# Cross attention: VectorE divides one unit's values ahead of an older batch's slot numbers

## The chip, the cores and the metric

One core of a Trainium2 chip runs the whole program. The metric is the device time in microseconds (us), as the median of three runs.

## The reference

Two decoder layers work on x of 8 batches x 256 tokens x 256 features, and on a context of 8 x 77 x 256. Each layer is: layer norm and self attention, layer norm and cross attention against the context, then a mixture of 8 experts. Cut to the cross attention of layer 0 and to the choice of experts that follows it:

```python
q, k, v = (query @ wq.T + bq), (key @ wk.T + bk), (value @ wv.T + bv)   # 16 heads of 16
attn = softmax(q @ k.T / sqrt(16)); ctx = attn @ v
x = x + ctx @ wo.T + bo
gate_logits = layernorm(x) @ Wg.T            # 8 experts
top_v, top_i = top_k(gate_logits, 2)         # two experts a token, gated by a softmax over the two
```

Layer 1 has the same cross attention with other weights, and its own top-2 experts.

## The kernel before, in words

The program is a row of stages: attention of layer 0 (L0a), cross attention (L0x), experts (L0f), and the same for layer 1 (L1a, L1x, L1f). The change is in `attention_crossed`, which writes both L0x and L1x. Each engine has a queue of instructions in an order written out by hand, and the engines meet only at semaphores.

**Units.** A batch b has two units, u = 2b (its *first* unit, c = 0) and u = 2b + 1 (its *second*, c = 1), each with 8 of the 16 heads; units run from 0 to 15. A unit goes through these steps, and all engines work on neighbouring units at once:

- TensorE makes scores (line 827). VectorE takes maxima (`maximum`, 468). TensorE turns them (837), and VectorE subtracts them from the queries (`shift`, 475).
- TensorE makes the scores again with keys as rows (`turned_scores`, 850). ScalarE takes exponentials (667). TensorE makes values and sums of the weights (`values`, 865) in the one bank `ps_o`.
- VectorE divides: `sums(u)` is a reciprocal (480) and a product (483), and frees `ps_o`.

TensorE's order in a first unit u is: scores(u+1), turning of u's maxima, the query product of b+1 (300), `r0` of b-2 (804), `values(u-1)`, `turned_scores(u)`. In a second unit it is: `r1` of b-2 (809), scores(u+1), turning, the value product of b+1 (288), the projection `o` of b-1 (797), transposes of b+2 (293), `turned_scores(u)`, `values(u-1)`, `r2` of b-2 (815). `o(b-1)` waits for `sums(2b-1)`, and `values(u)` for `sums(u-1)`.

**Routing.** Batches that are done are routed in the same queues, a part in each unit. VectorE's `choose` finds the two experts of a batch (514 to 529), `add` adds the projection to X and takes statistics (498 to 506), and `slots` counts tokens of each expert and makes the rows' slot numbers (536 to 546). GpSimd turns statistics into factors (255 to 258). ScalarE normalises the rows (`route_norm`, 627), and TensorE's `r0`, `r1` and `r2` make the logits and the counts. GpSimd's `send` (744) scatters a batch's rows into a table in device memory, in four indirect DMAs that wait for `slots`. Behind them in its queue is `bias` (725), one 128x512 addition in SBUF. `route_norm(b)` writes into the buffer that `send(b-2)` read, and waits until that scatter has landed.

**VectorE's order** is that of the function below. In a first unit of b >= 3 it is: `maximum(u+1)`, `shift(u)`, keys in u = 7 and 8 (192), statistics of b+2 (178 to 183, until b = 5), `slots(b-3)`, a piece of the experts' list, and `sums(u-1)`. The piece is at b = 3 a first count (L0x alone), at b = 5 the `order` of the experts (and in L0x `last_at_least`), at b = 6 and 7 a `snapshot`. When `order` is done, SyncE loads the first experts' weights.

Of the kernel before, what the change touches and what calls it, by code (L numbers as in the profile page):

```python
# [309 lines left out]
def attention_crossed(nc, name, env, wo, bo, first, route, experts, final):  # L310
# [10 lines left out]
    BANKS, PITCH, units, K_GROUPS, REST, TAIL, turns, at, events, by_scalar, keys_made, part, of, mid, START, END = first["order"]  # L321
# [22 lines left out]
    with ExitStack() as stack:  # L344
# [51 lines left out]
        def bank(*turn):  # L396
            if turn in TAIL:
                return ps_o if turn in (("r1", B - 2), ("r2", B - 2), ("r1", B - 1)) else ring[:, spare, :]
            return ring[:, at[turn] % BANKS, :]
# [40 lines left out]
        with nc.Block(no_gpsimd_drain=True) as block:  # L440
# [18 lines left out]
            def _(eng):  # L459
                def linked(ins):  # L460
                    first["linked_v"](eng, ins)

                def maximum(u):
                    eng.wait_ge(scores_done, u + 1)
                    for r0, i, n in runs(u):
                        src = ring[:, i:i + n, 0:4 * SC].rearrange("p n (g k) -> p n g k", k=SC)
                        dst = tops[u % 2][:, :, 2 * DH * r0:2 * DH * (r0 + n):2 * DH].rearrange("p g n -> p n g")
                        eng.tensor_reduce(dst, src, AX.X, ALU.max, negate=True).then_inc(max_done, 1)  # L468

                def shift(u):  # L470
                    b, c = part(u)
                    eng.wait_ge(tops_turned, u + 1)
                    eng.wait_ge(q_out, 3 * (b + 1))
                    q = q_m[b % 2][:, c, :, :]
                    eng.tensor_tensor(q, q, bank("m", u)[:, :].rearrange("p (w s) -> p w s", w=HALVES), ALU.add).then_inc(shifted, 1)

                def sums(u):
                    b, c = part(u)
                    eng.wait_ge(values_done, u + 1)
                    linked(eng.reciprocal(rsum[:, :], ps_o[:, S:2 * S]))  # L480
                    if c == 0 and b:
                        eng.wait_ge(projected, b)
                    eng.tensor_tensor(o_t[:, c, :], ps_o[:, 0:S], rsum[:, :], ALU.mult).then_inc(o_out, 1)
# [9 lines left out]
                def add(b):  # L493

                    eng.wait_ge(projected, b + 1)
                    eng.wait_ge(biased, b + 1)
                    xb = X[:, b * QT_N:(b + 1) * QT_N, :]
                    eng.tensor_tensor(xb, xb, bank("o", b)[:, :].rearrange("p (q d) -> p q d", q=QT_N), ALU.add).then_inc(added, 1)
                    eng.wait_ge(added, b + 1)
                    for q in range(QT_N):  # L500
                        ins = eng.bn_stats(r_stats[:, q, :], X[:, b * QT_N + q, :])
                    linked(ins)
                    if b:
                        eng.wait_ge(r_rstd_done, b)
                    for q in range(QT_N):
                        ins = eng.bn_aggr(r_mv[:, q, :], r_stats[:, q, :])
                    ins.then_inc(r_var_done, 1)

                def choose(b):

                    par = b % 2
                    wait_out(eng, "r1", b)
                    for q in range(QT_N):
                        ins = eng.max(top[:, q, :], logits[:, q, :])
                    linked(ins)
                    if b:
                        eng.wait_ge(odds_done, b)
                    eng.tensor_tensor(apart[:, :], top[:, :, 1], top[:, :, 0], ALU.subtract).then_inc(apart_done, 1)
                    for q in range(QT_N):
                        ins = eng.max_index(index[:, q, :], top[:, q, :], logits[:, q, :])  # L520
                    linked(ins)
                    linked(eng.tensor_copy(index_f[:, :, :], index[:, :, 0:TOP]))
                    for k in range(TOP):
                        ins = eng.tensor_tensor(chosen[:, k, :, :], route["experts"][:, :].unsqueeze(1).to_broadcast([P, QT_N, EXPERTS]),
                                                index_f[:, :, k].unsqueeze(2).to_broadcast([P, QT_N, EXPERTS]), ALU.is_equal)
                    linked(ins)
                    eng.tensor_tensor(both[:, :, :], chosen[:, 0, :, :], chosen[:, 1, :, :], ALU.add).then_inc(both_done, 1)
                    eng.tensor_copy(xr[:, par, :, FIRST_EXPERT], index_f[:, :, 0])
                    eng.tensor_copy(xr[:, par, :, TOKEN], route["from_end"][:, b * QT_N:(b + 1) * QT_N])

                def slots(b):

                    par, taken = b % 2, route["taken"]
                    eng.wait_ge(odds_done, b + 1)
                    gate = xr[:, par, :, GATE:GATE + TOP]
                    linked(eng.tensor_scalar(first_gate[:, :], odds[:, :], 1.0, None, ALU.add))
                    linked(eng.reciprocal(gate[:, :, 0], first_gate[:, :]))
                    eng.tensor_tensor(gate[:, :, 1], gate[:, :, 0], odds[:, :], ALU.mult)
                    wait_out(eng, "r2", b)
                    for q in range(QT_N):  # L540
                        eng.tensor_tensor(place[:, q, :], counts[:, 0, q, :], taken[:, :], ALU.add)
                        linked(eng.tensor_tensor(taken[:, :], counts[:, 1, q, :], taken[:, :], ALU.add))
                    linked(eng.tensor_tensor(picked[:, :, :, :], chosen[:, :, :, :],
                                             place[:, :, :].unsqueeze(1).to_broadcast([P, TOP, QT_N, EXPERTS]), ALU.mult))
                    linked(eng.tensor_reduce(slot_f[:, :, :], picked[:, :, :, :], AX.X, ALU.add))
                    eng.tensor_copy(slot_i[:, par, :, :], slot_f[:, :, :].rearrange("p k t -> p t k")).then_inc(slot_done, 1)
# [5 lines left out]
                for u in range(units):  # L552
                    b, c = part(u)
                    if u == 0:
                        shift(0)
                    if u + 1 < units:
                        maximum(u + 1)
                    if u:
                        shift(u)
                    for t in mid(u):  # L560
                        if t[0] == "k":
                            first["take_keys"](eng, t, bank(*t))
                    if c == 0:
                        if b + 2 < B:
                            first["statistics"](eng, b + 2)
                        if b >= 3:
                            slots(b - 3)
                            if b == 3 and not final:
                                experts["count_first"](eng)
                            if b - 3 == ORDER_BY:  # L570
                                experts["order"](eng)
                                if not final:
                                    experts["last_at_least"](eng)
                            for i, last in enumerate(FULL_BY):
                                if b - 3 == last:
                                    experts["snapshot"](eng, last)
                    else:
                        if b >= 2:
                            choose(b - 2)
                        if u == units - 1:  # L580
                            sums(u - 1)
                        if b >= 1:
                            add(b - 1)
                    if u and u < units - 1:
                        sums(u - 1)
                slots(B - 3)
                x["take_early"](0)
# [2204 lines left out]
```

## Time and profile before

| | |
|---|---|
| median of 3 runs | 1499.4 us (1499.39 to 1502.16) |
| the profiled execution's own time | 1493.69 us |
| its span, first to last instruction | 1492.0 us |
| mean granted TensorE clock | 0.991 |
| busy in the span: TensorE | 1419.1 us (95%) |
| busy in the span: VectorE | 754.9 us (51%) |
| busy in the span: ScalarE | 625.6 us (42%) |
| busy in the span: GpSimd | 493.2 us (33%) |

Shares are means over stages with different limits, so the two stages that the change touches have to be read for themselves. Batches 3 to 7 lie at about 261 to 343 us in L0x and at 1116 to 1198 us in L1x. A start in the rows is us from the span's start.

### The profile page before, as it was taken

The page shows a single profiled execution, that of the slowest core. Times are in us where ns is not written, and L with a number is a line of the kernel's source. Part 1 is how long each engine was busy: PE and PEld are TensorE (multiplying, and loading weights), DVE is VectorE, ACT ScalarE, POOL GpSimd, SP SyncE. Part 2 cuts the span into 40 slices and gives each one's busy share as a digit, 9 for nine tenths or more (in the row PEclk, how much of TensorE's full clock was granted, in tenths as well). Part 3 has the DMA queues.
Part 4 walks back from the last instruction along what each step waited for, and adds up shares of the span by engine and source line. Part 5 has one row for each costly group of instructions (what it writes and reads, how often), then busy time and mean ns, then how long its engine had stood idle before and what let it go on. Part 6 is the DMA issues. An engine that isn't in the chain of part 4 may idle for free. (4 is left out here: it accounts for less than half of the span.)

```text
span 1492.0 us, 33834 instructions
## 1 busy us (share of the span) xinstructions
PE 1419.1 (95%) x11400; PEld 1146.9 (77%) x11401; DVE 754.9 (51%) x2161; ACT 625.6 (42%) x1726; POOL 493.2 (33%) x758
## 2 busy tenths in 40 slices
PE   7999989989999999999999999999899999999998
PEld 5666666667999999967777777777666679999997
DVE  6777757997333333344444444444378962222222
ACT  3444446653122222245454554554366543333332
POOL 3555532445212212223323322333124452222222
PEclk9999999999999999999999999999899989999999
DMA  9930000152243333210000000000001522534332
GB/s 319 343 107 25 23 16 16 44 178 80 37 147 93 91 88 95 37 53 1 1 1 1 1 1 1 0 1 1 1 16 45 186 76 36 148 93 96 94 90 34
DMA packets 84464, 101.35 MB, mean 68 GB/s; under 512 B 11483, under 2 KB 77379, under 8 KB 84355
## 3 DMA queue, kind: packets, MB, share of 16 engines
q1 hardware_dynamic: 64643, 77.58, 16.3%
q0 software_dynamic: 13680, 17.19, 6.7%
q10 hardware_dynamic: 6032, 5.12, 1.0%
q8 instruction: 69, 1.13, 0.3%
q14 instruction: 40, 0.33, 0.1%
HBM read 57.51 MB, written 39.59 MB: 65 GB/s over the span
## 5 line engine op out<-in xcount | busy, mean ns | idle before, releaser
L1784 POOL TENSOR_TENSOR L1a_prob<-L1a_prob,L1a_rtot 128x1024 f32<-128x1024 f32 x64 | 121.1, 1892 | 277.4 <-DVE L1a_rtot L1657 277.4
L2313 PEld LDWEIGHTS L0x_ps<-L0f_rows_t,L0f_w_up 128*128 128x128 f32 x1584 | 182.0, 192 | 10.4 <-issue 9.0
L2313 PE MATMUL L0x_ps<-L0f_rows_t,L0f_w_up 128*128 128x128 f32 x1584 | 184.2, 276 | 5.6 <-issue 4.8
L2389 ACT ACTIVATE L1f_hid<-L1x_ps,L1f_b_up 128x128 f32<-128x128 f32 x296 | 92.8, 364 | 164.2 <-PE L1x_ps L2313 163.8
L2313 PEld LDWEIGHTS L1x_ps<-L1f_rows_t,L1f_w_up 128*128 128x128 f32 x1184 | 140.2, 194 | 3.4 <-issue 1.6
L2313 PE MATMUL L1x_ps<-L1f_rows_t,L1f_w_up 128*128 128x128 f32 x1184 | 141.1, 278 | 0.6 <-ACT L1f_rows_t L2373 0.6
L2322 PE MATMUL L1x_ps<-L1f_w_down,L1f_hid 128*128 128x256 f32 x592 | 135.8, 383 | 1.9 <-DVE wv L2491 1.9
L2257 POOL TENSOR_TENSOR turn<-eps 128x1 f32<-128x1 f32 x74 | 13.6, 184 | 374.3 <-DVE wv L2491 370.7
L1726 ACT ACTIVATE L1a_prob<-L1a_ps_s,L1a_nmax 128x256 f32<-128x256 f32 x256 | 118.4, 474 | 38.5 <-DVE L1a_nmax L1652 38.5
L2322 PEld LDWEIGHTS L1x_ps<-L1f_w_down,L1f_hid 128*128 128x128 f32 x592 | 110.7, 192 | 16.0 <-issue 2.1
L1287 POOL TENSOR_SCALAR_AFFINE_SELECT L0a_prob<-L0a_prob 128x128 f32<-128x128 f32 (+1 forms) x256 | 82.4, 362 | 90.7 <-ACT L0a_prob L1219 90.7
L2381 ACT ACTIVATE ctx_in<-L0x_ps 128x256 f32<-128x256 f32 x72 | 27.6, 384 | 181.5 <-PE L0x_ps L2313 181.4
L2322 PE MATMUL L0x_ps<-L0f_w_down,L0f_hid 128*128 128x256 f32 x432 | 99.4, 380 | 1.5 <-DVE L0f_hid L2478 1.5
L1652 DVE TENSOR_REDUCE L1a_nmax<-L1a_ps_s 128x2 f32<-128x512 f32 x128 | 79.4, 682 | 32.2 <-PE L1a_ps_s L1848 32.2
L1219 ACT ACTIVATE L0a_prob<-L0a_ps 128x384 f32<-128x384 f32 x128 | 52.4, 496 | 98.9 <-PE L0a_ps L1373 98.9
L2322 PEld LDWEIGHTS L0x_ps<-L0f_w_down,L0f_hid 128*128 128x128 f32 x432 | 79.3, 190 | 11.0 <-DVE L0f_hid L2478 1.7
L1862 PEld LDWEIGHTS L1a_ps_t<-ident,L1a_prob 128*128 128x128 f32 x500 | 59.6, 141 | 34.6 <-issue 26.3
L2478 DVE TENSOR_TENSOR L0f_hid<-ctx_in,L0x_ps 128x256 f32<-128x256 f32 x72 | 30.2, 421 | 104.6 <-ACT ctx_in L2381 104.6
L1862 PE MATMUL L1a_ps_t<-ident,L1a_prob 128*128 128x128 f32 x500 | 76.9, 276 | 3.3 <-DVE L1a_prob_t L1661 2.4
L1661 DVE COPY L1a_prob_t<-L1a_ps_t 128x512 f32<-128x512 f32 x63 | 42.9, 681 | 58.9 <-PE L1a_ps_t L1862 58.9
L1736 ACT ACTIVATE L1a_prob_t<-L1a_ps_t 128x512 f32<-128x512 f32 x62 | 37.1, 598 | 81.4 <-PE L1a_ps_t L1862 81.4
L2468 DVE TENSOR_SCALAR token<-L1f_from_end 128x1 int32<-128x1 f32 x37 | 5.7, 154 | 128.7 <-DMA out_dram<-wv,token 128.7
(490 smaller groups left out, 2794.9 us busy)
## 6 DMA issues: line engine op xcount, KB each, us to landing
expert_table<-zero SPq DMA_DIRECT2D x1, 16640.0 KB, 69.7
L0f_w_up<-in_w_dram SPq DMA_DIRECT2D x8, 1408.0 KB, 6.4
L1f_w_up<-in_w_dram SPq DMA_DIRECT2D x8, 1024.0 KB
L1f_w_down<-in_w_dram SPq DMA_DIRECT2D x8, 1024.0 KB
L0f_w_down<-in_w_dram SPq DMA_DIRECT2D x8, 768.0 KB, 8.3
L1f_rows<-expert_table SPq DMA_DIRECT2D x35, 130.0 KB
L0f_rows<-expert_table SPq DMA_DIRECT2D x32, 130.0 KB
sums<-X SPq DMA_DIRECT2D x8, 256.0 KB, 2.5
```

The lines of the kernel that those rows point to most:

```text
L1219: eng.activation(prob[u % 2][:, r, :, :], bank("p", u, r)[:, 0:KT * W].rearrange("p (t w) -> p t w", t=KT), ACT.Exp).then_inc(exp_done, 1)
L1287: ins = eng.affine_select(out=p, in_=p, compare_op=ALU.is_ge, fill=0.0, base=base, pattern=[[0, 2], [sign, n]], channel_multiplier=-sign)
L1652: eng.tensor_reduce(nmax[:, j % RING, :], src, AX.X, ALU.max, negate=True).then_inc(max_done, 1)
L1661: eng.tensor_copy(prob_t[s % 2][:, k, :], turn_bank(b, s, k)).then_inc(even_out, 1)
L1726: ins = eng.activation(prob[:, j % RING, q, :], ps_s[:, k, q * S:(q + 1) * S], ACT.Exp, bias=nmax[:, j % RING, q:q + 1], accum_out=total[: ...
L1736: eng.activation(prob_t[s % 2][:, k, :], turn_bank(b, s, k), ACT.Copy).then_inc(odd_out, 1)
L1784: eng.tensor_tensor(v, v, r.unsqueeze(2).to_broadcast([P, 2 * QT_N, S]), ALU.mult).then_inc(norm_done, 1)
L1862: ins = eng.transpose(out[:, o:o + P], prob[:, j % RING, q, c * P:(c + 1) * P], ident[:, :])
L2313: ins = eng.matmul(ps_h[c][:, o:o + P], w_up[par][:, t, w0:w0 + P], rows_t[:, t, :], start=(t == 0), stop=(t == DT - 1))
L2322: ins = eng.matmul(ps_y[:, 0:D], hid[:, c, k * P:(k + 1) * P], w_down[par][:, 2 * c + k, :], start=(c == 0 and k == 0), stop=(c == CHUNKS ...
L2389: ins = eng.activation(hid[:, c, k * P:(k + 1) * P], ps_h[c][:, k * P:(k + 1) * P], ACT.Gelu, bias=b_up[par][:, 2 * c + k:2 * c + k + 1])
L2478: ins = eng.tensor_tensor(hid[:, c, :], mid[:, c, :], ps_h[c][:, 2 * P:4 * P], ALU.mult)
```

## The change

In a first unit from b = 3 on, `sums(u-1)` comes ahead of `slots(b-3)` and the piece behind it. In batches 1 and 2 and in second units the order stays as it was. No instruction is added or taken away; the order changes in five units of each of the two stages.

```diff
                     if c == 0:
                         if b + 2 < B:
                             first["statistics"](eng, b + 2)
+                        if u:
+                            sums(u - 1)
                         if b >= 3:
                             slots(b - 3)
...
-                    if u and u < units - 1:
+                    if c == 1 and u < units - 1:
                         sums(u - 1)
```

## Rows read from the trace of the kernel before

**Rows 1.** Busy us (instructions) of PE, PEld, DVE, ACT, POOL; clock, DMA; batch 5

```profile
1149.00:1165.00 16.00, 14.89 (x171) 10.41 (x174) 15.17 (x52) 9.31 (x20) 7.92 (x13) 1.00 0.43 125
```

**Rows 2.** Line 483, who waited for it: us in total, times

```profile
  PE L0x_ps L797: 3.0, 2
...
  PE L1x_ps L797: 1.7, 2
```

**Rows 3.** Timeline, VectorE, L1x batch 3: start, us, instruction, idle before

```profile
1121.04 0.14 DVE L536 TENSOR_SCALAR L1x_first_gate<-L1x_odds 128x2 f32<-128x2 f32 x1
...
1122.49 0.17 DVE L546 CAST L1x_slot_i<-L1x_slot_f 128x4 int32<-128x4 f32 x1
...
1129.04 0.78 DVE L192 TENSOR_SCALAR L_shared<-L1x_ps,half_mask,L1x_k_bias 128x154 f32<-128x154 f32 x2 [2.09 <-PE L1x_ps L282]
...
1130.49 0.17 DVE L522 CAST L1x_index_f<-L1x_index 128x4 f32<-128x4 uint32 x1
```

**Rows 4.** Timeline, TensorE, L1x: the values of units 5, 9, 11 and 13

```profile
1120.74 1.05 PE L865 MATMUL L1x_ps_o<-L1x_prob,half_ones 77*32 77x256 f32 x16
...
1153.76 1.05 PE L865 MATMUL L1x_ps_o<-L1x_prob,half_ones 77*32 77x256 f32 x16
...
1170.35 1.05 PE L865 MATMUL L1x_ps_o<-L1x_prob,half_ones 77*32 77x256 f32 x16
...
1185.00 1.05 PE L865 MATMUL L1x_ps_o<-L1x_prob,half_ones 77*32 77x256 f32 x16
```

**Rows 5.** Timeline, VectorE, L1x batch 5: slots, sums, maximum, shift, a cast of choose

```profile
1154.30 0.13 DVE L536 TENSOR_SCALAR L1x_first_gate<-L1x_odds 128x2 f32<-128x2 f32 x1
...
1157.84 1.75 DVE L480 RECIPROCAL L1x_rsum<-L1x_ps_o 128x256 f32<-128x256 f32 x1
...
1159.97 1.50 DVE L468 TENSOR_REDUCE L1x_tops<-L1x_ps 128x4 f32<-128x308 f32 x2
1161.38 0.68 DVE L475 TENSOR_TENSOR L1x_q_m<-L1x_q_m,L1x_ps 128x512 f32<-128x512 f32 x1
...
1162.76 0.17 DVE L522 CAST L1x_index_f<-L1x_index 128x4 f32<-128x4 uint32 x1
```

**Rows 6.** Timeline, GpSimd, L1x: bias of batch 4; first send and bias of batch 6

```profile
1145.76 1.28 POOL L725 TENSOR_TENSOR X<-X,bo 128x512 f32<-128x512 f32 x1
...
1171.64 1.07 POOL L744 DMA_INDIRECT expert_table<-L1x_xr,L1x_slot_i  x1 [4.74 <-DVE L1x_slot_i L546]
...
1176.52 1.28 POOL L725 TENSOR_TENSOR X<-X,bo 128x512 f32<-128x512 f32 x1
```

**Rows 7.** Timeline, VectorE, L1x batch 4: the same cast of choose

```profile
1145.30 1.79 DVE L522 CAST L1x_index_f<-L1x_index 128x4 f32<-128x4 uint32 x1
```

**Rows 8.** Timeline, TensorE, L1x: r0 of batches 2 and 4; turned scores of 11, 13, 15

```profile
1135.89 0.63 PE L804 MATMUL L1x_ps<-ident,L1x_xr 128*128 128x128 f32 x4 [0.27 <-ACT L1x_xr L627]
...
1162.53 1.10 PE L850 MATMUL L1x_ps<-L1x_q_m,L_shared 32*77 32x256 f32 x16
...
1168.94 0.60 PE L804 MATMUL L1x_ps<-ident,L1x_xr 128*128 128x128 f32 x4
...
1177.59 1.10 PE L850 MATMUL L1x_ps<-L_shared 32*77 32x256 f32 x16
...
1191.34 1.10 PE L850 MATMUL L1x_ps<-L1x_q_m,L_shared 32*77 32x256 f32 x16
```

**Rows 9.** Timeline, ScalarE: the rows' normalisation of batch 4, in L1x and in L0x

```profile
1167.17 1.09 ACT L627 ACTIVATE L1x_xr<-X,L1x_r_shift_by,L1x_r_rstd 128x256 f32<-128x256 f32 x2 [0.89 <-DMA expert_table<-L1x_xr,L1x_slot_i]
...
312.13 1.09 ACT L627 ACTIVATE L0x_xr<-X,L0x_r_shift_by,L0x_r_rstd 128x256 f32<-128x256 f32 x2 [0.61 <-POOL L0x_r_shift_by L258]
```

**Rows 10.** Timeline, VectorE, L1x batch 6: slots, sums of unit 11, shift of unit 13

```profile
1169.71 0.16 DVE L536 TENSOR_SCALAR L1x_first_gate<-L1x_odds 128x2 f32<-128x2 f32 x1
...
1172.09 1.75 DVE L480 RECIPROCAL L1x_rsum<-L1x_ps_o 128x256 f32<-128x256 f32 x1
...
1175.89 0.68 DVE L475 TENSOR_TENSOR L_shared<-L_shared,L1x_ps 128x512 f32<-128x512 f32 x1
```

## The prediction, made before the changed kernel ran

> **What bounds the kernel now.** I read the table of busy time by stretch first. In batch 5 of L1x [rows 1] VectorE is busy for 15.17 of 16 us and TensorE for 14.89. Both are nearly full, so neither has room for a delay. VectorE's queue here is slots, order, sums, maximum, shift, with no idle time between them [rows 5]: it sets the pace, and what it delivers late TensorE waits for. Then I read who waited for the product of `sums`: TensorE's projection `o` did, twice in each stage, 3.0 us in L0x and 1.7 us in L1x [rows 2]. These are the waits that the change aims at. Last come the timelines of the four engines, with two questions. Are the values there when VectorE asks for them earlier? And what stands behind the work that is made later?
>
> **What the change moves.** It adds and removes nothing. Its first effect is `sums` ahead of slots. Its second is that slots, and all that hangs on it, come later: the four indirect DMAs on GpSimd's queue, GpSimd's `bias` behind them, `route_norm` on ScalarE (it waits for a scatter of two batches before), and at batch 5 SyncE's loads of weights. `maximum` and `shift` of the next unit stand behind slots and sums in either order, so they gain nothing; they lose whatever VectorE now idles while it waits for values that slots used to cover.
>
> The prices that recur are these. From the start of a sums to the next instruction VectorE takes 2.13 us (1157.84 to 1159.97) [rows 5]. Slots takes 1.62 us until the slot number is written (1121.04 to 1122.66) [rows 3]. Slots and order take 3.54 us (1154.30 to 1157.84) [rows 5], slots and snapshot 2.38 us (1169.71 to 1172.09) [rows 10]. The maximum before a shift is 1.41 us (1159.97 to 1161.38) [rows 5]. A first send starts 0.3 us after the slot number (written 1.64 us after 1169.71), and bias 4.88 us after that (1171.64 to 1176.52) [rows 6, 10]: 5.2 us from slot number to bias. VectorE starts a reciprocal 0.06 us after its values end, which is my estimate from the near coincidence of such pairs.
>
> **Batch 3, L1x.** The values of unit 5 end at 1121.79 [rows 4], VectorE is free at 1121.04 [rows 3]. It idles 0.8 us, and sums starts at 1121.85. Slots starts at 1123.98 and writes at 1125.6, where it was 1122.66: 2.9 us later. The 0.8 us itself costs nothing, since VectorE waited 2.09 us for a key product after this [rows 3]; without that cover it would cost 0.8. But bias moves to 1130.8 to 1132.1. A cast in batch 4 took 1.79 us instead of 0.17 [rows 3, 7]: it began 0.46 us ahead of the record of bias and ended 0.05 us behind its end (1145.76 + 1.28) [rows 6]. So GpSimd's addition holds small SBUF work of VectorE, from about half a microsecond before its record. In batch 3 the same cast stands at 1130.49 [rows 3], now inside such a stretch (1130.2 to 1132.1): 1.43 us lost. It sits ahead of `add`, and `add` leads over GpSimd and ScalarE to TensorE's r0(2), which already waited 0.27 us for it [rows 8]. TensorE enters batch 4 some 1.4 us late.
>
> The Trainium skill, "SBUF — State Buffer", section "Who interferes with whom", says that VectorE and GpSimd share a port pair under an exclusive lock, taken by whichever starts first, and that a cast or an operation with two SBUF inputs contends while one with at most one does not. The long cast agrees with the kinds it names, but by the records it started first and still waited. By the rule with recorded starts, the cast would pass here and the comparison behind it would be held, at nearly the same price.
>
> **Batch 4.** The old stall of 1.62 us (1.79 less 0.17) [rows 3, 7] goes, because bias moves behind `choose`. VectorE catches up, TensorE does not: it is dense here, and VectorE's lead ends in a wait for values. I take 1.45 us late for TensorE on entry to batch 5 (from below 0, if the cast of batch 3 is missed).
>
> **Batch 5, L1x.** The values of unit 9 ended at 1154.81 [rows 4], now at 1156.26. Sums starts at 1156.32, slots at 1158.45; behind slots and order maximum starts at 1162.0 and shift at 1163.4, ending at 1164.1. Turned scores of unit 11 started at 1162.53 [rows 8], now at 1164.15: 1.6 us late. The projection gets its operand early and no longer waits, but shift is the next thing late, and takes the gain. The slot number is written at 1160.07, bias is at 1165.2, and the cast of `choose` moves from 1162.76 [rows 5] to 1164.8, again inside the held stretch, until 1166.6. The scatter and the weight loads both move 4.1 us (the slot number from 1155.92, 1.62 us after 1154.30). ScalarE's normalisation of batch 4 ended a wait for that very scatter at 1167.17 [rows 9]; it moves to 1171.3. TensorE's r0(4) follows at 1172.5 (1.09 us, and 0.14 to start), where it was 1168.94 [rows 8]: 3.5 us late.
>
> **Batches 6 and 7, L1x.** The values of unit 11 ended at 1171.40 [rows 4], now at 1174.95. Sums starts at 1175.0, and behind it and 2.38 us of slots and snapshot come the maximum (1.35 us, one instruction now) and, at 1180.9, shift, where it was 1175.89 [rows 10]. It ends at 1181.5. Turned scores of unit 13 move from 1177.59 [rows 8] to 1181.65: 4.1 us. Up to here a held operation in batch 6 is saved, but TensorE sets the next values. In batch 7 r0(5) is late by 4.55 us, since bias holds GpSimd until then. So the values of unit 13 end at 1190.6 instead of 1186.05 [rows 4], sums starts at 1190.66, shift at 1195.2, and it ends at 1195.9. Turned scores of unit 15 start at 1195.95 instead of 1191.34 [rows 8]: **4.6 us** for L1x.
>
> **L0x.** The same steps give the same 1.45 at the entry and 1.6 at unit 11. In L0x the normalisation of batch 4 was released by GpSimd and not by the scatter [rows 9]. The late `add` (2.0 us of order and shift, 0.9 of a held operation) puts it 2.9 us late, and a shift of the scatter by 4.1 could at most put it 4.1 late. TensorE had about a microsecond of room, which leaves 2.1 to 3.2; I take 2.4, near the lower end, because that row shows no wait for the DMA. Unit 13 adds 0.5 as in L1x, unit 15 another 0.6: **3.5 us**. What follows each stage is dense TensorE work, which gives nothing back. I expect the later scatters before the early experts to be hidden.
>
> **Sum.** 3.5 + 4.6 = 8.1 us. The profiled execution's own time is 1493.69 us (span 1492.0), so it would be 1501.8. The runs' median lies 5.7 us above that execution, so the median becomes 1499.4 + 8.1 = **1507.5 us**, slower by 0.54%.
>
> **Rivals.**
> - *The cast of batch 3 escapes* (its margin to the start of the held stretch is 0.3 us). Then TensorE enters batch 5 on time, and the same steps end about 2.1 us late in L0x and 3.15 in L1x: 5.3 us, 1504.7. Against it: the stretch is 1.9 us long, and the operations behind the cast would fall into it.
> - *Scatter and bias are absorbed*, so only the idle time for values stays: 0.2 us at unit 11 and 0.5 at unit 13 in each stage, 1.5 us, 1500.9. For it: four operations of batch 4 to 7 that were held are freed. Against it: the DMA wait in L1x [rows 9] is already open, and its source moves.
> - *Faster: the projection's wait is last.* If shift were in time, the waits of 3.0 and 1.7 us [rows 2] would go, 4.7 us: 1494.7. It decides if shift(11) ends before the transposes ahead of turned scores do. Before, shift ended at 1162.06 and the product started at 1162.53 [rows 5, 8], a room of 0.47 us; with the wait gone TensorE asks 0.9 us sooner, and VectorE comes at least 0.5 us later, since it idles for values. Only a freed operation of 1.6 us could tip that.
> - *Worse:* further casts are held, or late scatters reach the early experts' rows. Another 3 us: 1510.5.
>
> **Chances.** My forecast with its neighbourhood (6.5 to 9.5) has 0.40, the escape 0.24, absorbed 0.14, faster 0.10, worse 0.12. The range from 1500.5 to 1511 leaves out the faster case and half of the worse one. A measurement here tells 0.2%, 3.0 us, from no change. Slower by more: forecast, escape and worse, less some of the escape, 0.75. Within: 0.15. Faster by more: 0.10.
>
> **What the profile after would show.** In each first unit of batch 3 to 7 VectorE idles for line 865 ahead of line 480, 0.2 to 1.9 us. `o` waits for line 483 no more, and turned scores (850) wait for line 475 in units 11, 13 and 15. The cast at line 522 is long in batches 3 and 5 and short in batch 4. Line 627 of batch 4 in L1x waits for the scatter some 4 us later than before. The prediction is wrong if VectorE is at line 475 of unit 11 no later than before, or if its held operations vanish altogether.

## The result, and the profile after

The changed kernel took 1512.4 us as the median of six runs (1510.43 to 1514.5), the kernel before 1500.78 us beside it. The ratio is 1.0069, with a 95% interval of 1.0046 to 1.0092: slower by 0.7%. The forecast was 1507.5 us with a range to 1511. The sign and the place of the loss are as forecast, the median lies 1.4 us above the range.

The profiled execution took 1512.99 us, span and clock are these (before: 1492.0 us, 0.991):

```profile
core 0: 1511.3 us, clock 0.983
```

**The wait that the change aims at.** The product of `sums` (line 483), who waited for it, in total us and times; it answers to [rows 2]:

```profile
  PE L1x_ps_o L867: 2.3, 1
  PE L0x_ps_o L867: 2.3, 1
```

The projection `o` is gone from the list. The one wait left in each stage is that of `values`, line 867 (865 before; lines behind the change are two further on), at the very end of the stage. The kernel before had that one too, 1.62 us in each stage where it is 2.3 us now.

**VectorE in L1x**, from batch 3 to batch 5 (start, us, instruction, idle time before it):

```profile
1126.09 1.76 DVE L480 RECIPROCAL L1x_rsum<-L1x_ps_o 128x256 f32<-128x256 f32 x1 [1.28 <-PE L1x_ps_o L867]
...
1140.62 1.67 DVE L522 CAST L1x_index_f<-L1x_index 128x4 f32<-128x4 uint32 x1
...
1142.85 0.68 DVE L498 TENSOR_TENSOR X<-X,L1x_ps 128x512 f32<-128x512 f32 x1
```

They answer to [rows 3]. VectorE now idles for the values ahead of a sums, and the cast of batch 3, 0.17 us before, is held to 1.67 us. The GpSimd addition beside it:

```profile
1139.97 0.96 POOL L746 DMA_INDIRECT expert_table<-L1x_xr,L1x_slot_i  x1 [0.30 <-issue]
1140.96 1.29 POOL L727 TENSOR_TENSOR X<-X,bo 128x512 f32<-128x512 f32 x1
```

The cast starts 0.34 us ahead of the addition's record and ends 0.04 us behind its end (1142.25), as in [rows 6, 7].

**TensorE in L1x**, its waits from batch 4 on:

```profile
1143.59 0.61 PE L817 MATMUL L1x_ps<-L1x_both,before 128*128 128x16 f32 x2 [1.18 <-DVE X L498]
...
1177.70 1.10 PE L852 MATMUL L1x_ps<-L1x_q_m,L_shared 32*77 32x256 f32 x16 [1.05 <-DVE L1x_q_m L475]
...
1185.95 0.63 PE L806 MATMUL L1x_ps<-ident,L1x_xr 128*128 128x128 f32 x4 [1.29 <-ACT L1x_xr L629]
...
1211.97 1.10 PE L852 MATMUL L1x_ps<-L1x_q_m,L_shared 32*77 32x256 f32 x16 [0.93 <-DVE L1x_q_m L475]
```

`r2` waits for the add behind the held cast, turned scores wait for shift at units 11 and 15, `r0(4)` waits for the normalised rows. These rows answer to [rows 8]. The normalisation itself, in L0x and in L1x, answers to [rows 9]:

```profile
317.83 1.09 ACT L629 ACTIVATE L0x_xr<-X,L0x_r_shift_by,L0x_r_rstd 128x256 f32<-128x256 f32 x2 [1.27 <-DMA expert_table<-L0x_xr,L0x_slot_i]
...
1184.72 1.09 ACT L629 ACTIVATE L1x_xr<-X,L1x_r_shift_by,L1x_r_rstd 128x256 f32<-128x256 f32 x2 [3.15 <-DMA expert_table<-L1x_xr,L1x_slot_i]
```

In both stages ScalarE's last wait is now the one for the scatter.

**What no step of the forecast has.** The busy times by stretch show the granted clock in the column after POOL (the columns are those of [rows 1]):

```profile
230.00:310.70 80.70, 74.53 (x833) 52.87 (x837) 68.22 (x178) 50.71 (x107) 29.64 (x53) 1.00 0.11 35
310.70:320.90 10.20, 10.20 (x74) 6.49 (x67) 7.53 (x21) 3.43 (x8) 1.93 (x5) 0.50 1.01 383
320.90:344.80 23.90, 21.34 (x239) 14.15 (x238) 18.14 (x61) 11.59 (x25) 7.58 (x10) 1.00 0.24 78
1096.30:1143.60 47.30, 44.87 (x517) 31.67 (x517) 38.81 (x91) 30.76 (x63) 14.32 (x27) 1.00 0.07 24
1143.60:1150.40 6.80, 6.80 (x33) 5.63 (x34) 4.98 (x8) 1.29 (x3) 1.34 (x4) 0.50 0.13 41
1150.40:1188.00 37.60, 34.18 (x389) 23.80 (x391) 31.08 (x93) 23.41 (x48) 15.76 (x26) 1.00 0.38 119
1188.00:1198.20 10.20, 10.20 (x63) 7.12 (x54) 8.11 (x28) 2.82 (x7) 4.35 (x5) 0.50 0.61 205
```

For 10.2 us of L0x and for 6.8 and 10.2 us of L1x TensorE had 1.2 GHz, where it has 2.4 GHz in the rest. In the profiled execution of the kernel before, these two stages, up to the turned scores of unit 15, ran at 1.00 throughout. That is one execution, with a mean clock of 0.991; other runs of that kernel lie between 0.980 and 0.997. The low stretches begin behind waits of TensorE: the one at 1143.6 with the end of r2's wait of 1.18 us, the one at 310.7 after waits of 1.59 and 0.73 us, the one at 1188.0 some 2 us after a wait of 1.29 us. What half the clock means is seen on one group of products, the query product, in the stretch at 1143.6:

```profile
1146.80 3.62 PE L300 MATMUL L1x_ps<-L1x_xt,wq 128*128 128x256 f32 x8
```

Eight products of this shape take 1.89 us at the full clock; the projection's row at 1158.34, in the experiments below, shows it.

**Where the time went.** From the first sums of a stage to the turned scores of unit 15 the kernel before took 106.4 us in L0x and 105.1 in L1x, the changed one 114.9 and 115.6. That is 8.5 and 10.5 of the 19.3 us between the two spans; the rest of the program adds 0.3. Two executions of unlike clock (0.991 and 0.983) can't tell how much of it is the schedule.

### The profile page after: what moved, and what is told of

It is laid out like the page before. It is cut to its first block and busy times, and to the rows that moved or that the text cites. A ratio compares the mean times of both kernels' runs of the same rounds, so it can differ in the third digit from the quotient of the medians.

```text
span 1511.3 us, 33834 instructions
## 1 busy us (share of the span) xinstructions
PE 1433.3 (95%) x11400; PEld 1154.8 (76%) x11401; DVE 753.7 (50%) x2161; ACT 626.1 (41%) x1726; POOL 494.6 (33%) x758
## 3 DMA queue, kind: packets, MB, share of 16 engines
q8 instruction: 69, 1.13, 0.3%
```

## Telling schedule from clock

All runs but the six of the kernel before in the first call list a time and a mean granted clock, 260 runs in all. The runs of the kernel before alone reach from 1485 to 1511 us, and their time follows the clock. A straight line was fitted, with a constant for each kernel in each call (a group of versions measured together on one chip) and one slope for all. By it a run takes 1.14 us more for each 0.001 of clock that it lacks (standard error 0.02), and what is left over scatters by 1.1 us. The differences between those constants are the times at equal clock below. They compare kernels of one call, on one chip: by the fit the kernel before had 1482.2 us at full clock on one chip and 1487.1 to 1487.8 on the three others. The first row of the table is weaker than the rest. The kernel before lists no clock in that call, so the next call's constant of another chip, 1487.5, stands in; with the 1482.2 of the one fast chip the same row would be 12.6. The ± of the other rows is the standard error of the fit.

| kernel | runs | ratio, 95% interval | mean clock, before's | at equal clock, us |
|---|---|---|---|---|
| changed, first | 6 | 1.0069 (1.0046 to 1.0092) | 0.9847, not listed | +7.3, by a stand-in |
| changed, second | 6 | 1.0121 (1.0096 to 1.0147) | 0.9852, 0.9926 | +8.8 ± 0.6 |
| changed, third | 12 | 1.0073 (1.0049 to 1.0096) | 0.9863, 0.9880 | +8.2 ± 0.4 |
| in L0x alone | 12 | 1.0042 (1.002 to 1.0065) | 0.9849, 0.9864 | +4.1 ± 0.4 |
| in L1x alone | 12 | 1.0011 (0.9988 to 1.0034) | 0.9878, 0.9864 | +4.8 ± 0.4 |
| in batch 3 alone | 12 | 1.0022 (0.9996 to 1.0047) | 0.9884, 0.9864 | +4.0 ± 0.4 |
| from batch 4 on | 12 | 1.003 (1.0005 to 1.0054) | 0.9873, 0.9864 | +5.5 ± 0.4 |
| changed, bias first | 12 | 1.0049 (1.0028 to 1.0069) | 0.9851, 0.9883 | +5.4 ± 0.4 |
| before, bias first | 12 | 1.0014 (0.9989 to 1.004) | 0.9891, 0.9883 | +3.4 ± 0.4 |
| changed, idle products | 6 | 1.0092 (1.0064 to 1.0119) | 0.9895, 0.9883 | +16.3 ± 0.5 |
| before, idle products | 6 | 1.013 (1.0101 to 1.0159) | 0.9873, 0.9883 | +20.9 ± 0.5 |
| sums behind slots | 12 | 1.0008 (0.9992 to 1.0024) | 0.9911, 0.9926 | -0.8 ± 0.4 |
| and the piece behind shift | 6 | 1.0061 (1.0038 to 1.0083) | 0.9855, 0.9926 | +0.9 ± 0.6 |
| changed, piece behind shift | 6 | 1.0123 (1.0102 to 1.0144) | 0.9822, 0.9926 | +6.2 ± 0.6 |
| piece behind choose | 12 | 1.0033 (1.0007 to 1.006) | 0.9849, 0.9880 | +2.8 ± 0.4 |
| piece behind add | 12 | 1.0032 (1.0007 to 1.0057) | 0.9847, 0.9880 | -0.4 ± 0.4 |

## The experiments

### One stage at a time

```diff
-                        if u:
+                        if u and b >= 3 and not final:
                             sums(u - 1)
```

(For the other stage it is `and final`. The condition on the later `sums(u - 1)` is changed to match.)

> The change in L0x alone. Two theories stand. Cascade: each stage pays for itself by held casts, idle time of VectorE and late shifts, so L0x alone costs about half of the change's 10 to 12 us, 5 to 6 us, its last sums come 10 us later than before and L1x takes as long as before. Clock: the extra beyond my 8 us is TensorE's clock, which falls to the half inside the stage; then the half-clock stretch near 310 us is here too and none between 1090 and 1190 us. If instead the execution of before that was profiled was only a lucky one for the clock, the ratio is below 1.002.

> The change in L1x alone. Cascade: 5 to 6 us more, none of it in L0x. Half-clock stretches inside L1x (near batches 4 and 6) as in the changed kernel, none inside L0x. L0x alone and L1x alone should add up to the whole change within 2 us.

At equal clock L0x costs 4.1 us where the forecast had 3.5, and L1x 4.8 where it had 4.6. That is a little under the 5 to 6 us which the expectations gave each. The two together make 8.9, the whole change 8.2 and 8.8 in the calls that list both clocks: the stages add up, and both terms of the sum are near their size. The ratio of the L1x version does not show its 4.8 us, since its clock was 0.0014 higher than that of the kernel before, which is worth 1.6 us. The expectations of the clock came out in part. With the change in L0x alone a stretch of 6.8 us at half clock begins at 277.40, with the end of a wait of 1.55 us of `r2` that the kernel before did not have; none lies near 310 us or inside L1x. With the change in L1x alone there is one of 3.4 us in batch 3 of L1x, but also one of 13.65 us in L0x, where nothing was changed.

### Batch 3 against the rest

```diff
-                        if u:
+                        if u and b == 3:
                             sums(u - 1)
```

> Sums ahead of slots in batch 3 alone, in both stages. Held cast: the cast of choose at line 522 in batch 3 takes 1.7 to 1.8 us instead of 0.17, TensorE is 1.4 us late from there and VectorE gives nothing back, so each stage costs 1.4 to 3 us, 3 to 6 in all. Rival, that idle time for values is the cost: it is covered here by the wait for the key product, so no more than 0.5 us in all.

> Sums ahead of slots in batches 4 to 7, not in 3. Cascade: without the held cast of batch 3 TensorE enters batch 5 on time, the steps give 2.1 us in L0x and 3.15 in L1x, 5.3 us, and up to 9 if the clock falls in batches 5 and 6 all the same. If the held cast of batch 3 set off everything, at most 2 us.

From batch 4 on the change costs 5.5 us, close to the 5.3 us of the rival in which the cast of batch 3 escapes. Here it did escape, since batch 3 was left alone. Batch 3 by itself costs 4.0, in the expected range of 3 to 6; the forecast's sum gave it 2.8 (8.1 less 5.3). Its cast is held for 1.66 us in L1x. The cast of batch 4, which the whole change frees, is held here as well (1.78 us at 1150.31, 0.17 in the changed kernel). The two parts make 9.5, more than the whole, and fit that.

### GpSimd's addition out of the way

```diff
+                        if b in (3, 4, 5, 6, 7):
+                            bias(b)
                         if b >= 3:
                             send(b - 3)
                     else:
-                        bias(b)
+                        if b not in (3, 4, 5, 6, 7):
+                            bias(b)
```

(In the kernel before the same is done in batches 4, 6 and 7 alone, where its operations were held.)

> The changed kernel with GpSimd's bias ahead of its send in batches 3 to 7, so that the 128x512 addition runs while VectorE is in a reciprocal from PSUM. Hold theory: the casts of choose are short in every batch, the loss at batch 3 is gone, and of the change's 10 to 12 us only 2 to 4 stay (idle time for values, late shift, late scatter). Rival, that late scatter and shift are the cost: 7 us or more stay.

> The kernel before with bias ahead of send in batches 4, 6 and 7 alone, where its choose was held for 1.6, 0.9 and 1.9 us. If these holds cost it something, 1 to 3 us less than before; by my steps TensorE's own work limits the gain to 0.5 us in batch 4 and nothing later, so 0.5 to 1.5 us less, inside what can be told.

The same casts of choose in L1x, in batches 3 to 6 of the changed kernel with bias first:

```profile
1125.03 0.17 DVE L522 CAST L1x_index_f<-L1x_index 128x4 f32<-128x4 uint32 x1
...
1143.33 0.28 DVE L522 CAST L1x_index_f<-L1x_index 128x4 f32<-128x4 uint32 x1
...
1158.97 0.17 DVE L522 CAST L1x_index_f<-L1x_index 128x4 f32<-128x4 uint32 x1
...
1177.49 0.42 DVE L522 CAST L1x_index_f<-L1x_index 128x4 f32<-128x4 uint32 x1
```

None takes 1.7 us any more, with the same instruction in VectorE's queue and only GpSimd's order changed. So GpSimd's addition is what holds the cast. The change then costs 5.4 us instead of 8.4 (the mean of its second and third measurements, weighted by precision, ± 0.3), so the move gives back 3.0 us, compared across chips. The expectations had 2 to 4 us left if holds were the cost, and 7 or more if late scatter and shift were; 5.4 lies between them, so each has a part. In the kernel before, the same move was expected to gain 0.5 to 1.5 us and costs 3.4. Bias ahead of the scatters has a price of its own then, and the 3.0 us are what is left after it, so they do not measure the holds alone. That the price comes from the indirect DMAs, which stand behind bias in this order, is argued and not shown.

### Idle products where TensorE waits

```diff
+                    if t in (("r0", B - 4), ("r0", B - 3), ("r2", 1)):
+                        idle_products(eng, out, ident, 8)
...
+                        if B - 4 <= t[1] < B - 1:
+                            idle_products(eng, ps_o, ident, 8)
```

Eight products of 128x128 whose results are overwritten, ahead of `r2(1)`, `r0(4)` and `r0(5)` and behind `o` of batches 4 to 6, in both stages.

> The changed kernel with 8 idle products of TensorE at six places where it waits (before r2 of batch 1, before r0 of batches 4 and 5, behind o of batches 4, 5 and 6), some 0.9 us each. Clock theory: inside L0x and L1x the granted clock stays full, the half-clock stretches of 10 us near batch 5 and 6 are gone, and the kernel is 2 to 5 us below the changed one. Rival, that the clock is not what makes it longer: the same as the changed kernel or slower by the products' own time, up to 4 us.

> Control: the same idle products in the kernel before. It had no half clock inside these stages, so it can only lose: 0 to 8 us (12 places of 0.9 us, less the projection's waits of 3.0 and 1.7 us). If it gains, its other runs than the profiled one lost the clock there too.

Busy times by stretch, the changed kernel with idle products, L0x and L1x from the first sums to unit 15:

```profile
230.20:345.20 115.00, 110.71 (x1236) 82.16 (x1236) 94.77 (x265) 65.36 (x141) 39.63 (x68) 1.00 0.22 76
1095.70:1209.80 114.10, 110.73 (x1240) 82.20 (x1240) 93.78 (x259) 63.77 (x135) 39.53 (x68) 1.00 0.24 77
```

The low stretches inside the two stages are gone in this execution, and the mean clock of its runs, 0.9895, is the highest among the versions that contain the whole change (0.9822 to 0.9863 without the products). That fits a low clock that goes with TensorE's idle time there. The control does not fit as well. In the kernel before, the products were expected to cost at most 8 us, and they cost 20.9 at equal clock; its mean clock was 0.9873 against 0.9883. Its profile has 3.4 us at half clock near 310 us and 6.8 us from about 328 us on, in a stage that ran at 1.00 throughout in the profile without them. Nor are the products a remedy: they stand in front of work that is due, and cost the changed kernel 8 us at equal clock, where 2 to 5 us less than the changed kernel were expected.

### Where the projection's wait goes

Five orders of VectorE's queue, each with one more thing out of the way. In the first, slots stay first and sums go ahead of the piece of the experts' list alone:

```diff
                         if b >= 3:
                             slots(b - 3)
+                        if u:
+                            sums(u - 1)
+                        if b >= 3:
                             if b == 3 and not final:
                                 experts["count_first"](eng)
```

> Slots, then sums, then the piece of the experts' list (first count, order, snapshot): the slot number, the scatters and bias keep their old times, and only the piece goes behind sums, in both stages. The product of sums is ready earlier by the piece, 1.9 us at batch 5 and 0.75 at batches 6 and 7. Theory (shift is the next thing late, and it stands behind the same work as before): the projection's waits go, shift(11), shift(13) and shift(15) stay where they were to 0.3 us, and at equal clock the time is that of the kernel before to 1 us. Rival, the projection's wait was the last one: the waits of 3.0 and 1.7 us are gained, -4.7 us. Rival, sums ahead of anything costs: +1 to +3 us.

TensorE in L1x in that version, with VectorE's rows around it:

```profile
1158.34 1.89 PE L800 MATMUL L1x_ps<-wo,L1x_o_t 128*128 128x256 f32 x8
...
1161.55 1.10 PE L853 MATMUL L1x_ps<-L1x_q_m,L_shared 32*77 32x256 f32 x16 [0.88 <-DVE L1x_q_m L475]
```

```profile
1154.91 0.17 DVE L546 CAST L1x_slot_i<-L1x_slot_f 128x4 int32<-128x4 f32 x1
...
1159.31 1.50 DVE L468 TENSOR_REDUCE L1x_tops<-L1x_ps 128x4 f32<-128x308 f32 x2
1160.73 0.68 DVE L475 TENSOR_TENSOR L1x_q_m<-L1x_q_m,L1x_ps 128x512 f32<-128x512 f32 x1
```

In the kernel before, the projection waited 0.86 us here for line 483 (one of the two waits of [rows 2]):

```profile
1160.20 1.97 PE L797 MATMUL L1x_ps<-wo,L1x_o_t 128*128 128x256 f32 x8 [0.86 <-DVE L1x_o_t L483]
```

Now it does not wait, and 1.3 us behind its end the turned scores wait 0.88 us for line 475. The slot number is written at 1154.91, as early in the stage as before, and maximum and shift follow the piece as they did; the wait has moved in full. In L0x the projection's wait of 2.12 us became two, 1.22 for the maximum that frees a bank for the transposes and 0.73 behind them. Only the other wait, 0.89 us in batch 7, found room: there turned scores of unit 15 are 1.0 us earlier in each stage. At equal clock all of it is worth 0.8 ± 0.4 us, and the ratio, 1.0008 (0.9992 to 1.0024), can't tell it from the kernel before.

In the second the piece goes behind maximum and shift too, so that shift gains as well:

```diff
                     else:
+                        if b >= 3:
+                            if b == 3 and not final:
+                                experts["count_first"](eng)
+                            if b - 3 == ORDER_BY:
+                                experts["order"](eng)
...
                         if b >= 2:
                             choose(b - 2)
```

> Slots, then sums, and the piece of the experts' list goes behind maximum and shift of the next unit, ahead of choose. Now shift(11) is earlier by 1.9 us as well as the product of sums, and shift(13), shift(15) by 0.75 us. Theory (projection and shift both set TensorE's pace, one behind the other): now the waits of 3.0 and 1.7 us are gained at least in part, -2 to -4.7 us at equal clock, and less if TensorE's next wait, for scores or the normalised rows, takes its place. Rival, TensorE's own work is the bound here and its waits only move: within 1 us of the kernel before. Choose and what hangs on it come 1.9 us later at batch 5; if that is what counts, slower by 1 to 2 us.

Against the kernel before, each measured from the stage's first sums, the turned scores of unit 11 are 1.1 us early in L1x and 2.2 in L0x. Those of unit 12 are 1.7 us late in both. TensorE between the two, and what VectorE did meanwhile:

```profile
1172.39 0.37 PE L818 MATMUL L1x_ps<-L1x_both,before 128*128 128x16 f32 x2 [0.80 <-DVE L1x_both L527]
```

```profile
1167.77 1.92 DVE L2030 TENSOR_TENSOR wq<-L1r_by_place 128x64 f32<-128x64 f32 x1
...
1172.07 0.17 DVE L527 TENSOR_TENSOR L1x_both<-L1x_chosen 128x16 f32<-128x16 f32 x1
```

`r2` waits 0.80 us for choose, which stands behind the piece (2.07 us in L0x). An instruction of the piece that takes 0.22 us in the changed kernel, at 305.35 us, is held to 1.92. My theory of a gain of 2 to 4.7 us fell; the rival, that the wait only moves, holds with +0.9 ± 0.6.

The third is the change itself with the piece behind shift.

> The change with the piece of the experts' list moved behind maximum and shift of the next unit. The scatters and bias are as late as in the changed kernel (2.1 to 4.1 us), but shift(11) comes 1.9 us sooner than there, shift(13) and shift(15) 0.75 us sooner. If the late slot number and what hangs on it (scatter, normalised rows, held operations) is what costs at batches 6 and 7, and shift only at unit 11, it stays at +4.5 to +6.5 us at equal clock. If the late shift itself were most of it, +1 to +3 us.

It costs 6.2 ± 0.6 us, within the 4.5 to 6.5 of the theory. Taking 1.9 us off the late shift of unit 11 gives back 2.6 of the 8.8 us that the change costs in the same call. The rest stays with the late slot number and what hangs on it (scatter, rows, held casts); this run does not tell these apart.

In the last two the piece goes behind choose, and behind choose and add.

> As the version with the piece of the experts' list behind maximum and shift, but behind choose too, ahead of add. There r2 waited 0.80 us for choose's last product after shift had gained 1.1 to 2.2 us; here choose keeps its old place. Theory (VectorE's queue is full in batch 5, 15.17 of 16 us, and whatever is put off is what TensorE waits for next): add is 1.9 us late, and the next wait is for rows that are normalised from it; within 1 us of the kernel before at equal clock. Rival, choose was the only one that TensorE needed at once: -2 to -3 us.

> The same with the piece behind add too, as the last work of the second unit before its sums. Choose and add keep their old times, and there was 0.32 us of idle time ahead of these sums. Theory: sums(10) is 1.6 us late, and with it maximum(13), so scores or values wait; within 1 us of the kernel before at equal clock. Rival: shift(13) has room, since it is one unit further on, and the gain of the earlier shift(11) stays: -1 to -3 us, and the version beats both kernels.

Behind choose it is +2.8 ± 0.4 us, which neither theory had. Its profile has, in L0x, a wait of `r0` for the normalised rows of 2.01 us at 333.91 (1.12 in the kernel before) and one of turned scores for line 475 of 1.63 at 327.06. At 312.25 TensorE also idles 2.65 us for "issue", which means that the profile shows nothing it waits for. In L1x the same wait of `r0` is as before, 1.15 against 1.13, and TensorE idles 1.40 and 1.04 us for "issue". These idle times stay unexplained. Behind add it is -0.4 ± 0.4, as the theory had it: `values` now wait for line 483 (1.95 us at 315.97, 0.69 at 1174.84). Its ratio, 1.0032, is above 1 all the same, since its mean clock is 0.9847 against 0.9880. No version of the five beats the kernel before by more than 0.2%.

### The changed kernel again

> The changed kernel once more, unchanged. In all runs so far, some 150 of ten kernels, a kernel's time follows its own mean granted TensorE clock by 1.16 us for each 0.001. By that line the change's schedule costs 7.2 us and the rest of its 10 to 11 us is a lower clock (0.9847 against 0.9871). Theory: at equal clock it is again 6.5 to 8 us longer than the kernel before, and its mean clock is again lower by 0.001 to 0.004. Rival, that the lower clock was chance: the same 7 us at equal clock, and a mean clock within 0.001 of the kernel before's, so that the medians differ by 7 to 8 us.

> The changed kernel a third time, for its clock. So far its mean granted clock was 0.9847 and 0.9852 on two chips, and that of the kernel before 0.9864 to 0.9926. If the late units lower the clock, this gives 0.984 to 0.986 again, below the kernel before in the same call by at least 0.001, and +7 to +8.5 us at equal clock. If the clock is the chip's affair, its mean is within 0.001 of the kernel before's.

At equal clock the change costs 8.8 and 8.2 us, and the clock is 0.9852 and 0.9863, below the kernel before's by 0.0074 and 0.0017. The price of the schedule repeats; 8.8 is a little above the expected 6.5 to 8. By the scatter of the runs the first of the two clock differences is clear, and the second is less than twice its standard error. The mean clock of the changed kernel stays within 0.0016 in three calls, while that of the kernel before moves between 0.9864 and 0.9926 over four; so the clock's part of the difference, 2 to 8 us, depends on the chip or the hour.

The third one's L1x ran at 1.00 from the first sums to unit 15, so its profile can be laid on the forecast without the clock. TensorE:

```profile
1150.03 1.10 PE L852 MATMUL L1x_ps<-L_shared 32*77 32x256 f32 x16
...
1174.49 1.10 PE L852 MATMUL L1x_ps<-L1x_q_m,L_shared 32*77 32x256 f32 x16 [1.05 <-DVE L1x_q_m L475]
...
1182.45 0.63 PE L806 MATMUL L1x_ps<-ident,L1x_xr 128*128 128x128 f32 x4 [1.01 <-ACT L1x_xr L629]
...
1191.62 1.10 PE L852 MATMUL L1x_ps<-L_shared 32*77 32x256 f32 x16 [0.42 <-issue]
...
1205.86 0.46 PE L852 MATMUL L1x_ps<-L1x_q_m,L_shared 32*77 32x256 f32 x4 [0.93 <-DVE L1x_q_m L475]
```

The stage began 9.48 us later than in the profile before (first reciprocal at 1095.69 and 1086.21). With that taken off and the starts of [rows 8] subtracted, unit 11 is late by 2.5 us (forecast 1.6), `r0(4)` by 4.0 (3.5), unit 13 by 4.55 (4.1), unit 15 by 5.0 (4.6). Unit 8, whose start before was 1139.06, is late by 1.5 (1.45). Unit 13 has a wait of 0.42 us that the profile puts down to nothing; its shift ends at 1191.57, 0.05 us ahead of it.

L0x can be compared in the same way in the second measurement, which ran at the full clock there until about 335 us. Its start was 0.33 us later. Unit 8 is late by 1.7 us (forecast 1.45), unit 11 by 1.8 (1.6), `r0(4)`, at 317.92, by 3.4 (2.4), and unit 13, at 327.08, by 3.9 (2.9).

## Why the prediction was right, and where it was wrong

- **The projection's wait is not the last one: right.** Line 483 holds up `o` no more, line 475 holds up turned scores by 0.93 to 1.05 us at units 11 and 15 of L1x, and by 0.42 at unit 13, as forecast. The version with sums ahead of the piece alone shows it with everything else in place.
- **The cast of batch 3 is held, that of batch 4 freed, that of batch 5 held again: right in L1x.** 1.67 us in batch 3 here, and 1.66, 0.17 and 1.80 in batches 3 to 5 of the third measurement. In L0x batch 5 holds an operation of the same routine instead, 1.06 us at line 518. With bias first 3.0 us of the price go.
- **TensorE is late by 1.45 behind batch 3: right**, 1.5 at unit 8 in the execution with a full clock.
- **Unit 11 late by 1.6: too little by 0.9 in L1x.** TensorE's lateness did not stay at 1.45. In that execution the values of unit 8 themselves came late: from the turned scores of unit 9 to `r2` behind these values it is 3.84 us, where it was 2.90 in the kernel before. So unit 10 was late by 2.2 already, and sums and shift follow the values (rows below). The 0.28 us in the rows is all that the profile shows as idle, and it names no releaser; what the 0.94 us are stays open. They are there in L1x of five more profiles with sums ahead of slots in batch 4 (3.83 to 4.25 us), and absent in two, the second measurement and the change with the piece behind shift (2.89 and 2.90). In L0x there was one wait more that I had not looked for, the transposes of the batch after next, which need a bank that `maximum(12)` frees: 1.59 us at 308.83.

```profile
1156.72 1.10 PE L852 MATMUL L1x_ps<-L_shared 32*77 32x256 f32 x16
...
1159.95 0.68 PE L867 MATMUL L1x_ps_o<-L1x_prob,half_ones 77*32 77x256 f32 x5 [0.28 <-issue]
1160.56 0.39 PE L817 MATMUL L1x_ps<-L1x_both,before 128*128 128x16 f32 x2
```

- **The scatter leads to `r0(4)`: right in L1x, too small in L0x**, where I had it only as a bound and took 2.4 us. There too ScalarE's idle time ends with the scatter (1.27 us in the first profile), `r0(4)` is 3.4 us late in the second measurement, and L0x costs 4.1 instead of 3.5.
- **The sum, 8.1 us: right at equal clock**, where the two measurements beside a kernel before with a listed clock give 8.8 and 8.2, mean 8.4 ± 0.3. How close it came is in part luck. In L1x the excess of 0.9 us at unit 11 had shrunk to 0.4 at unit 15, and batch 3 alone cost 4.0 where the sum gave it 2.8.
- **"So the median becomes 1499.4 + 8.1": this step failed.** It takes for granted that the clock stays, and so puts the clock's term at nothing without a reason. The runs of the changed kernel had 0.9847, and those of the kernel before in later calls 0.9864 to 0.9926. The median of the kernel before beside it was also 1.4 us above the one I was shown, so the difference in that call is 11.6 us where 8.1 was forecast. With the new median the schedule's 7.3 makes 1508.1, and a clock lower by 0.0017 to 0.0036 (against 0.9864 to 0.9883, the calls with much the same time before) adds 1.9 to 4.1: 1510.0 to 1512.2, where 1512.4 was measured. This reckoning takes the first call's chip to be like the three slower ones, since the kernel before lists no clock there, so how the 11.6 us of that call divide is an estimate. The later calls show the step failing without it: 8.2 and 8.8 us are the schedule's, and 1.9 and 8.4 more go with a clock lower by 0.0017 and 0.0074. The range had no term for the clock, and ended at 1511.

That the low clock comes with the change's own waits is supported by three things: low stretches begin behind new waits in the first profile and in that of L0x alone, with idle products in these places they are gone from the changed kernel, and in three calls its mean clock was much the same. It is not settled, and four things speak against it. The version with the change in L1x alone had 13.65 us of low clock in its unchanged L0x, from 331.2 us on. The version from batch 4 on costs 5.5 us, and its clock was not below that of the kernel before (0.9873 against 0.9864). The version with the piece behind add costs nothing at equal clock and had 0.9847 against 0.9880. And in the kernel before, idle products did not raise the clock. What the runs show is that the clock differs between versions and between calls by as much as the change is worth; why it fell with this change stays open.

## What to carry to other kernels

Where two engines are both over 90% busy in a stretch, a wait that the profile names is where their lateness happens to surface. Making its operand early moves it to the next thing that stands behind the same work; ask for each consumer in order, what is the next one to be late. Reordering has a second price: what was hidden under the work that moved (here an addition of another engine beside small casts, and a scatter two batches away) comes out in new places. And before a difference under 1% is explained, plot each run's time against its granted clock.

## What the runs showed of the hardware

**The spread of the runs goes with the clock.** It is 1.14 us for 0.001 over 260 runs, with 1.1 us left over. In a 1500 us span, 0.001 of the mean clock is 3 us at half clock, so by the fit one microsecond at half clock goes with 0.38 us of time here. Laid on the three profiles of the changed kernel this brings unlike ones together. From the first sums to unit 15, L0x took 8.5, 7.7 and 5.9 us longer than before, with 10.2, 9.3 and 3.4 us at half clock: less 0.38 of these, 4.6, 4.2 and 4.6. L1x took 10.5, 7.5 and 5.0 us longer, with 17.0, 10.2 and none at half clock: 4.0, 3.6 and 5.0.

**GpSimd's hold begins ahead of its record.** The held cast starts 0.34 us before the record of the addition and still waits for its end, here as in [rows 6, 7]. By the Trainium skill ("SBUF — State Buffer", "Who interferes with whom") the engine that starts first keeps the port. By the records the later one had it; either one of the two starts at another time than its record says, or the rule is not kept. The forecast went by the rows, and the held casts in L1x came out as the rows had it.

**Two engines that wake together, late.** In some executions VectorE and ScalarE stand idle for 3 us in a stretch that no edit touches, and go on within 0.15 us of each other. This is L1x of the version with the change in L0x alone:

```profile
1187.95 1.44 DVE L468 TENSOR_REDUCE L1x_tops<-L1x_ps 128x16 f32<-128x1232 f32 x1 [3.19 <-DMA L0a_valued<-L0a_both]
```

```profile
1188.07 0.38 ACT L245 ACTIVATE L1x_v_s<-L1x_ps 77x256 f32<-77x256 f32 x1 [2.91 <-remote]
```

```profile
1184.12 0.81 PE L829 MATMUL L1x_ps<-L_shared,L1x_q_raw 32*128 32x154 f32 x16 [0.25 <-issue]
...
1185.35 1.03 PE L288 MATMUL L1x_ps<-wv,ct 128*77 128x256 f32 x4
```

By the kernel's code what they need are the scores of line 829, ended at 1184.93, and the product of line 288, ended at 1186.38. The releasers that the profile names, a DMA of another stage and "remote", are not what these instructions wait for. The profile before has no such pair, but others have, as L0x at 323.83 and 323.95 in the kernel before with bias first. Here the turned scores behind it waited 1.94 us for line 475, so it costs about 2 us where it happens. What it is stays open.
